# Graph attention over 2048 nodes: dense masked attention replaced by attention over gathered edges

## The reference, cut to what matters

```python
h  = relu(layernorm(x))                            # no scale or bias
hs = layer_norm(h, ln1)                            # source rows
ht = layer_norm(h_target, ln1)                     # target rows
q = (ht @ Wq + bq) / sqrt(32); k = hs @ Wk + bk; v = hs @ Wv + bv
logits = einsum('thd,shd->hts', q, k);  logits = where(adj != 0, logits, -1e30)
ctx  = softmax(logits) @ v                         # per head, 2048 x 256
ht   = ht + ctx @ Wo + bo
ht   = layer_norm(ht, ln2)
out  = x + ht + gelu(ht @ W1) @ W2                 # tanh form of gelu
```

## Time and profile before

| | before |
|---|---|
| median of 3 runs | 491.26 us (490.76 to 491.69) |
| profiled execution, span | 488.1 us |
| instructions | 10628 |
| PE busy | 472.1 us, 97% |
| DVE busy | 418.4 us, 86% |
| ACT busy | 376.5 us, 77% |
| POOL busy | 305.6 us, 63% |
| moved by DMA | 46.93 MB |

### The profile page before, as it was taken

How to read it: one execution, slowest core, us unless ns; L and a number is a source line. 1 busy time by engine, 2 the same in 40 slices (tenths; PEclk the granted TensorE clock), 3 DMA queues, 4 the chain that set the end, 5 groups by cost and what they waited for, 6 DMA issues and landing times.

```text
span 488.1 us, 10628 instructions
## 1 busy us (share of the span) xinstructions
PE 472.1 (97%) x4366; PEld 243.2 (50%) x4366; DVE 418.4 (86%) x631; ACT 376.5 (77%) x462; POOL 305.6 (63%) x152
## 2 busy tenths in 40 slices
PE   3999989999999999999999999999999999999995
PEld 1557533343333333343333333343435888888884
DVE  6889499999999999999999999999997977566243
ACT  4887979998998998998998998999995571727150
POOL 1000019977998999999999998999998300000000
PEclk9999999999999999999999999999999999999999
DMA  8997879925432673232763400500000100202021
GB/s 231 243 217 133 157 216 385 346 47 109 172 69 47 76 173 58 44 52 50 77 177 57 77 2 3 186 35 1 2 2 1 46 33 13 87 1 86 1 87 45
DMA packets 53775, 46.93 MB, mean 96 GB/s; under 512 B 35486, under 2 KB 46652, under 8 KB 53212
## 3 DMA queue, kind: packets, MB, share of 16 engines
q1 hardware_dynamic: 51216, 37.30, 28.7%
q0 software_dynamic: 2480, 8.92, 10.4%
q10 hardware_dynamic: 28, 0.01, 0.0%
HBM read 31.93 MB, written 14.81 MB: 96 GB/s over the span
## 4 chain that ended last, share of the span: by engine, by line
PE 72%; DVE 11%; issue 9%; ACT 4%; POOL 3%; DMA 1%; DVEq 0%; POOLq 0%
PE acc L1434 18%; PE slot L1419 16%; PE acc L1452 8%; DVE probs L1044 8%; PE slot L1536 3%; PE slot L1534 3%; PE slot L1535 3%; PE slot L1322 3%; PE acc L1571 2%; PE acc L1573 2%; PE acc L1572 2%; PE slot L1485 2%; POOL added_up L554 2%; DVE stats L865 1%; PE slot L1342 1%
## 5 line engine op out<-in xcount | busy, mean ns | idle before, releaser
L1044 DVE SCALAR_TENSOR_TENSOR probs<-maskT,slot 128x1024 f32<-128x1024 uint16 x256 | 298.0, 1217 | 6.1 <-PE slot L1419 5.7
L759 ACT ACTIVATE probs<-probs 128x1024 f32<-128x1024 f32 x256 | 266.8, 1057 | 22.3 <-DVE probs L1044 4.8
L554 POOL TENSOR_TENSOR added_up<-added_up,probs 128x1024 f32<-128x1024 f32 x96 | 226.8, 2411 | 0.2
L1434 PE MATMUL acc<-probs,V 128*32 128x512 f32 x1024 | 136.3, 604 | 1.8 <-DVE q_lo_staged L970 1.8
L1452 PE MATMUL acc<-probs,ones 128*32 128x256 f32 x1024 | 77.0, 379 | 0.0
L1452 PEld LDWEIGHTS acc<-probs,ones 128*32 128x32 f32 x1024 | 33.3, 110 | 72.8 <-issue 71.2
L1419 PE MATMUL slot<-q_hi,k_hi 32*128 32x512 f32 x512 | 64.4, 493 | 0.9 <-DVE probs L1044 0.3
L823 ACT ACTIVATE g_full<-slot 128x512 f32<-128x512 f32 x32 | 19.3, 602 | 45.2 <-issue 30.0
L1419 PEld LDWEIGHTS slot<-q_hi,k_hi 32*128 32x128 f32 x512 | 24.5, 181 | 59.1 <-DVE probs L1044 54.4
L551 POOL TENSOR_TENSOR added_up<-probs 128x1024 f32<-128x1024 f32 x16 | 38.1, 2406 | 24.9 <-ACT probs L759 15.0
L1419 PE MATMUL slot<-q_lo,k_hi 32*128 32x512 f32 x512 | 51.8, 391 | 0.0
(11 more groups left out here) (144 smaller groups left out, 496.6 us busy)
## 6 DMA issues: line engine op xcount, KB each, us to landing
adj_raw<-in_adj POOLq DMA_DIRECT2D x16, 512.0 KB, 5.5
htn<-in_L_gnn_h_target SPq DMA_DIRECT2D x4, 512.0 KB, 7.4
ht_saved<-htn SPq DMA_DIRECT2D x1, 2048.0 KB, 8.1
k_hi_saved<-k_hi SPq DMA_DIRECT2D x1, 2048.0 KB, 10.2
k_lo_saved<-k_lo SPq DMA_DIRECT2D x1, 2048.0 KB, 14.5
v_saved<-V SPq DMA_DIRECT2D x1, 2048.0 KB, 8.9
inverse<-inverse_saved SPq DMA_DIRECT2D x8, 256.0 KB
maskT<-in_L_gnn_W SPq DMA_DIRECT2D x2, 1024.0 KB, 6.4
```

The source lines that it names most:

```text
L554: nc.gpsimd.tensor_tensor(added_up[:, pair], added_up[:, pair], at(i), ALU.add).then_inc(added, 1)
L759: nc.scalar.activation(p, p, ACT.Exp).then_inc(exped, 1)
L1044: nc.vector.scalar_tensor_tensor(out=probs[:, u % RING], in0=m, scalar=-HALF_EDGE, in1=slot[u % SLOTS][:], op0=ALU.add, op1=ALU.min).then_ ...
L1434: mm = pe.matmul(acc[HD * j:HD * j + HD, 0, :], V[:, i, h * HD:(h + 1) * HD], probs[:, (PAIRS * k + j // 2) % RING, j % 2, :], start=(i == 0),
```

## The change

The names in the diff: P = 128, SLOTS = 11, KEYS = 24, REST = 13, RING = 2, WIDE = 264, ST = 16 tiles of 128 targets, NP = 8 pairs of tiles, ROUNDS = 20.

Keys and values are projected with rows in the partitions, joined to rows of 512 floats, and stored in HBM (`kv_saved`); queries stay in SBUF (`q_rows`). All products are plain fp32; the split parts go. The mask, its transposes and the dense scores go.

Per pair of tiles the adjacency becomes a list of sources: ACT squares it in place and counts it (`square`), PE packs 16 blocks of 128 columns as powers of two into one word per column (`put_in_words`), DVE takes the top exponent three times to turn a word into keys (`find_levels`), and sorts the 24 largest keys of a row with `max` of eight at a time and `match_replace` (`rank_keys`). A key's bits give the source's row (`make_index`). A row's first 11 sources are its slots. What is beyond them is moved to any of 128 shared lanes of the tile, one lane a source, through small products with a matrix of owners (`share_a`, `make_offsets`, `share_b`, `move_shared`, `share_c`).

Per tile POOL issues 12 indexed transfers of 128 rows of 2 KB (`gather`: 11 near, 1 far). From the third tile on an empty slot's index lies outside of the table, and its row isn't moved. Each round n then does the following. Every function named is one stream's part.

```diff
+            def gather(n):
+                if n < 2:
+                    for parity in range(2):
+                        pool.wait_ge(kv_stored[parity], 16 * NCH // 2)
+                else:
+                    pool.wait_ge(far_weighed, n - 1)
+                pool.wait_ge(indexed, 2 * (n // 2) + 2)
+                for s in range(SLOTS):
+                    pool.indirect_dma_start(
+                        out=near[:, n % RING, s, :], out_offset=None, in_=kv_saved,
...
+                pool.wait_ge(shared, SHARE_STEPS * (n // 2) + 13)
+                pool.indirect_dma_start(
+                    out=far[:, n % RING, :], out_offset=None, in_=kv_saved,
...
+            for n in range(ROUNDS):
+                if n + 1 < ST:
+                    gather(n + 1)
+                if n + FIRST_ADJ < ST:
+                    load_adj(n + FIRST_ADJ)
+                e = widened_in(n + 1)
+                if e is not None:
+                    root_pair(e)
...
+            def exponentials(n):
+                act.wait_ge(scored, SCORE_STEPS * (n + 1))
...
+                nc.scalar.activation(weights, logits[:].rearrange("p s h -> p (s h)"), ACT.Exp).then_inc(exped, 1)
+                nc.scalar.activation(values[:, :, D:WIDE], logits[:], ACT.Exp).then_inc(exped, 1)
...
+            for n in range(ROUNDS):
+                if n + FIRST_SQUARES < ST:
+                    square(n + FIRST_SQUARES)
+                if n < ST:
+                    exponentials(n)
+                if n + 1 < ST:
+                    place_query(n + 1)
+                e = widened_in(n)
+                if e is not None:
+                    norm_pair(e)
+                    gelu(e, (0, 1))
+                if 0 < n <= ST:
+                    copy_context(n - 1)
+                if e is not None:
+                    gelu(e, (2, 3))
+                if 0 < n <= ST:
+                    copy_y(n - 1)
...
+            def score(n):
...
+                nc.vector.tensor_tensor(products[:], near[:, n % RING, :, 0:D],
+                                        query_ps[:, None, :].to_broadcast([P, SLOTS, D]), ALU.mult).then_inc(scored, 1)
...
+                nc.vector.tensor_reduce(logits[:].rearrange("p s h -> p (s h)"),
+                                        products[:].rearrange("p s (h i) -> p (s h) i", i=HD), AX_X, ALU.add
+                                        ).then_inc(scored, 1)
...
+            def weigh(n):
...
+                nc.vector.tensor_tensor(values[:, :, 0:D].rearrange("p s (h i) -> p s h i", i=HD),
+                                        near[:, n % RING, :, D:2 * D].rearrange("p s (h i) -> p s h i", i=HD),
...
+            for n in range(ROUNDS):
+                if n < ST:
+                    score(n)
+                    far_score(n)
+                if 0 < n <= ST:
+                    divide(n - 1)
+                e = finished_in(n)
+                if e is not None:
+                    finish(e)
+                e = ranked_in(n)
+                if e is not None:
+                    find_levels(e)
+                    rank_keys(e)
+                    make_index(e)
+                    share_a(e)
+                e = shared_in(n)
+                if e is not None:
+                    share_b(e)
+                if n < ST:
+                    weigh(n)
+                if e is not None:
+                    share_c(e)
+                if 0 < n <= ST:
+                    measure(n - 1)
+                if n == ST:
+                    test_ranges()
                     make_flag()
...
+            def sum_up(n):
...
+                for s in range(SLOTS):
+                    pe.matmul(acc, ident[:], values[:, s, :], start=(s == 0), stop=False)
...
+                pe.matmul(acc, owner_T[:, n // 2 % 2, n % 2, :], far_values[:], start=False, stop=True
+                          ).then_inc(summed_up, 1)
...
+            for n in range(ROUNDS):
+                if 0 < n <= ST:
+                    sum_up(n - 1)
+                e = widened_in(n)
+                if e is not None:
+                    turn_y(e)
+                    widen(e, (0, 1))
+                o = narrowed_in(n)
+                if o is not None:
+                    narrow(o, 0)
+                if 0 < n <= ST:
+                    turn_context(n - 1)
+                s = shared_in(n)
+                if s is not None:
+                    move_shared(s)
+                if n + 1 < ST:
+                    spread_query(n + 1)
+                if 0 < n <= ST:
+                    attend(n - 1)
+                if e is not None:
+                    widen(e, (2, 3))
+                if o is not None:
+                    narrow(o, 1)
+                w = worded_in(n)
+                if w is not None:
+                    put_in_words(w)
```

The start changes with it. PE's `project(c)` makes keys and values tile by tile into two alternating PSUM places each, which ACT (`values_out`) and DVE (`keys_out`) empty. Pairs 0 and 1 are ranked before round 0, with the target rows' work in between:

```diff
             rectify_chunk(2)
+            source_affine(1)
             source_root(2)
             normalise_source(2)
+            values_out(1)
...
+            target_root(0)
+            values_out(3)
+            square(0)
+            square(1)
             normalise_target(0)
             target_root(1)
             normalise_target(1)
             target_affine(0)
+            square(2)
+            square(3)
             target_root(2)
+            normalise_target(2)
             target_affine(1)
             target_root(3)
+            normalise_target(3)
             target_affine(2)
+            square(4)
             target_affine(3)
+            place_query(0)
...
+            keys_out(3)
             target_scale(0)
+            find_levels(0)
+            rank_keys(0)
+            make_index(0)
+            share_a(0)
             target_stats(1)
...
             target_scale(3)
+            find_levels(1)
+            rank_keys(1)
+            make_index(1)
+            share_a(1)
+            queries_out(2)
+            queries_out(3)
```

More of the change, by code:

```diff
@@ new lines, in graph_attention @@
+        squared = sem("squared")
+        worded = sem("worded")
+        levels = sem("levels")
+        ranked = sem("ranked")
+        indexed = sem("indexed")
+        bounded = sem("bounded")
+        shared = sem("shared")
+        offset_made = sem("offset_made")
+        moved_made = sem("moved_made")
+        near_in = [sem(f"near_in{i}") for i in range(RING)]
+        far_in = [sem(f"far_in{i}") for i in range(RING)]
+        query_in = sem("query_in")
+        far_query_in = sem("far_query_in")
@@ L672, in values_out, with source_affine @@
-            def values_out(c):
-                act.wait_ge(v_projected, c + 1)
-                nc.scalar.copy(V[:, rows_of(c), :], slot4[2]).then_inc(v_out, 1)
+            def source_affine(c):
+                act.wait_ge(x_turned, c + 1)
+                if c == 0:
+                    act.wait_ge(columns_made, 1)
+                if c >= 2:
+                    act.wait_ge(kv_projected, TILES * (c - 1))
+                for d in range(DC):
+                    nc.scalar.activation(hsT[:, c % 2, d, :], wide[:, d, :], ACT.Identity, bias=beta1[:, d:d + 1],
+                                         scale=gamma1[:, d:d + 1]).then_inc(x_affine, 1)
@@ new lines, in values_out @@
+            def values_out(c):
+                if c == 0:
+                    act.wait_ge(nodes_made, 1)
+                if c >= 2:
+                    act.wait_ge(kv_stored[c % 2], 16)
+                for t in range(TILES):
+                    n = c * TILES + t
+                    act.wait_ge(kv_projected, n + 1)
+                    nc.scalar.activation(kv_out[:, c % 2, t, D:2 * D], turned[:, n % 2, 0:D], ACT.Copy,
+                                         scale=nodes[:, n:n + 1]).then_inc(v_out, 1)
@@ new lines, in target_affine @@
+                if c >= 2:
+                    act.wait_ge(q_projected, 2 * (c - 1))
+                for d in range(DC):
+                    nc.scalar.activation(htT[:, c % 2, d, :], wide[:, d, :], ACT.Identity, bias=beta1[:, d:d + 1],
+                                         scale=gamma1[:, d:d + 1]).then_inc(t_affine, 1)
+                for d in range(DC):
+                    nc.scalar.activation(ht2[:, d, cols_of(c)], wide[:, d, :], ACT.Identity,
+                                         bias=rest_col[:, d:d + 1], scale=gamma1[:, d:d + 1]).then_inc(t_affine, 1)
@@ L701, in _ @@
             act.wait_ge(made, 2)
-            nc.scalar.activation(warm[:], ones[:, 0:1], ACT.Sqrt).then_inc(warmed, 1)
+            nc.scalar.activation(warm[:], ident[:, 0:1], ACT.Sqrt).then_inc(warmed, 1)
             rectify_half(0)
@@ new lines, in gelu, with copy_context @@
+            def gelu(e, parts):
+                for f in parts:
+                    act.wait_ge(widened, FC // 2 * e + f + 1)
+                    if e and f == 0:
+                        act.wait_ge(narrowed, 2 * e)
+                    nc.scalar.activation(hidden[:, 2 * f:2 * f + 2, :],
+                                         wide[:, f % 2, :].rearrange("p (f t) -> p f t", f=2), ACT.Gelu_apprx_tanh
```

(19 more changed lines are left out.)

1713 lines of the change are left out of this document (734 added, 979 removed).

## The result

The changed kernel takes 522.0 us (520.1 to 522.7, four runs) against 491.0 (490.3 to 491.7, four runs) before: a ratio of 1.063, 95% interval 1.060 to 1.065. It is slower. The forecast was 462 within 425 to 500. Of its three terms the start was laid at 127 and came at 129 us (first `score`), the end at 35 and came at 36, the rounds at 297 and came at 354. All of the miss lies in the rounds, where the single operations of DVE and ACT cost about what was laid.

The account below looks back on a forecast made before the run. PE (97% busy) and DVE (86%) were taken to bound the old kernel together, its dense steps costing 297 us of PE. Start 127 + rounds 297 + end 35 = 459 us span, plus 3.2 gives 462, range 425 to 500.

Parts of the forecast that it names:

- the start: Everything before the first `score`: source and query projections, ranking of the first pairs, first gathers; laid at 127 us.
- the end: The tail from the last `weigh` to the final store; laid at 35 us.
- the rounds: Rounds 0 to 15 together, even ones at 15.3 and odd ones at 22.3 us; laid at 297 us.
- 11 g + 2 < 16.1 means g < 1.28 costs nothing: POOL's gather: with g us per indexed transfer, taken as 1.1, rows land before `score` needs them, at no cost.
- rival B: POOL sets the round: above 1.28 us per indexed transfer rounds lengthen, 483 us total at 1.5; chance 0.22.
- beneath DVE, if the clock holds: PE's work in the rounds: 31.7 us a pair of rounds, less than DVE's 37.4, at full clock.
- rival C: PE's clock falls in odd-round waits: 8 us more on the chain, seven times, 518 us total; chance 0.12.
- The odd chain: Odd round's sequence across ACT, PE and DVE from `score` to `measure`, ending at 22.3 us, level with DVE's 22.1.
- ACT's exponentials come at 6.3: Odd round: ACT's exponentials start 6.3 us in, when DVE's `score` is done, and end at 7.7.
- The 3.2 us put on top of the span: Difference between the old kernel's span, 488.1, and median run, 491.3, added to the forecast span of 459 us.
- Rival E: Each ACT table switch costs a load and as long again: 1.4 us, 13 times, 18 more, 480; chance 0.05.
- Rival D: Start and chain are shorter than laid: 3 us less an odd round, 10 less of the start, 430; chance 0.16.

Follow-up runs that it names:

- the fill: The changed kernel without indexed transfers from tile 2 on, plus unread identity products where PE idles in odd rounds from 5 on; 471.6 us, 0.960.
- nogather: The changed kernel without the indexed transfers of tiles 2 to 15, later tiles reusing the rows of tiles 0 and 1; 479.9 us, 0.976.
- root_in_ten: root_in_burst with SLOTS 10 instead of 11, so 11 indexed transfers a tile; 467.0 us, 0.953.
- root_in_burst: norm_first's order, with two transfers of an even tile's burst issued before POOL's `root_pair` and ten after; 480.7 us, 0.979.
- no_rows: The changed kernel with all indexed transfers issued, but from tile 2 on bounded so that almost no bytes move; 515.7 us, 1.051.
- norm_first: The changed kernel with the odd round's normalising put before ACT's exponentials and `turn_y` before PE's `sum_up`; 515.4 us, 1.052.
- root_in_pause: root_in_burst with POOL starting the burst for tile 15 only when that for tile 14 has landed; 480.6 us, 0.978.

## Why the prediction was wrong

**The step that failed** is POOL's: "11 g + 2 < 16.1 means g < 1.28 costs nothing". It asked only whether the rows are there when `score` wants them. They are, at a pitch of 1.31 (laid 1.1), where rival B's own formula would add some 4 us and the traces show no wait. But the issue had a second cost that no row before could show, a hold of PE's signals to other engines: 42 us between the measured times with and without the transfers, 44 of the rounds' 57 (354 less 310). No rival had it; B took POOL's time as POOL's alone.

**The other 13 us** (310 less 297) are "beneath DVE, if the clock holds". With the clock kept by the fill, the rounds came to 297, the number laid. That it agrees to the us is luck, since the parts differ: even rounds 14.9 for 15.3, full odd ones 23.1 for 22.3, and rounds 0, 1 and 14 shorter by 0.9 to 1.4. So rival C was real, with a third of its price: 2.7 us an odd round, not 8. In the changed kernel itself round 7's clock is 0.91. From 283.74 on it is 0.53 for 1.6 us, near the lower of its two levels, and the 16 instructions that start there take 5.41 us, for 3.62 at the upper level. The Trainium skill's page "TensorE: Matmul & The Clock Gate", Part 1, has an idle array fall to half; the trace agrees, after gaps of 2.1 and 1.1 us.

**The odd chain** was laid with one wait left out. "ACT's exponentials come at 6.3" overlooks that they write into `values`, which `sum_up` reads, so that they cannot start before it ends: 8.2 in `nogather`, 11.5 in the changed kernel (round 7 of both). That a chain laid from `score` on must begin with PE at rest was a second fault: PE carries 2.5 us (`nogather`) to 5.9 us of the even round over.

**Right**: the start and the end within 2 us, of the start with some luck, since it holds a hold too: the last copy of the queries comes 1.7 us behind PE's last product in the changed kernel, while the burst for tile 1 runs. The products' durations, and nearly the reduces'; bf16 products (16 in 1.9 us). The 3.2 us put on top of the span was too much: the profiled execution took 521.4 us with a span of 519.7, 1.7 more. Rival E is dead: a table load is 1.28 and the next instruction follows at once (in `root_in_ten` a load at 268.86, the gelu at 270.16). The Trainium skill's page "ScalarE: Activation LUTs", section "What ACT_TABLE_LOAD costs", would have 2.66; the measurement decides. Rival D did not come: the start was 2 us longer, not shorter.

**The chance** of slower was put at 0.18. The upper end of the range, 500, allowed for the unknown time of an instruction that no row showed, but not for an unknown effect of it on others, and B, C and the rest had been priced only one at a time.

What stays open: what inside the core makes the hold, and what sets its onset. The ends of PE's products are modelled in the profile, so the traces cannot tell a late signal from a product that itself completed late. In all runs, copies of `context` and `y` whose products ended less than 10 us into a burst were late by 1.8 us at most; of those more than 12 us into one, about two in three were late, by 1.2 to 6.5 us, and the others by less than 1, among them those of `root_in_burst`. The second gelu of round 13, 15 us into its run (at 424.9), was not late either. Whether a run of plain transfers as long as 15 us would hold too was not tried, nor a single transfer with several indices a row.

## What to carry to other kernels

An instruction that no trace has shown has two unknowns, its own time and what it does to its neighbours; take it out, or issue it and move nothing, before building a schedule on it. Long runs of indexed transfers on POOL should be placed where no other engine waits for PE: start them right behind the last such wait, keep them short, and put POOL's own small work into them. When two edits each bring nothing, look whether a loop joins them before dropping both: here 7 and 1 us alone were 41 together.

## What the hardware showed that was not expected

Bursts of twelve indexed transfers (1.01 us each, 0.30 between) held PE's signals to ACT and DVE by up to 6.5 us, and by 13 us in a run of 24 (from 429.3, the middle of `widen`'s second half in round 13, to 442.5); with nearly no bytes moved (`no_rows`) as well. In the changed kernel most of them came 1.5 to 1.9 us after the last transfer. That is no rule: in round 13 of `no_rows` and `norm_first` the held gelu started 4.3 and 7.0 us before the run of 24 was over. Signals between DVE and ACT were not seen to be late. Late in a run of 24, PE's own products came one by one, some 1.4 us apart, close to POOL's pitch of 1.31. And the first `score` came anywhere from 129 to 135 us in traces of kernels whose start is the same. Part of that is the same hold: the last copy of the queries came 1.4 to 3.1 us behind PE's last product in 15 traces and 0.04 us behind it in the three of `root_in_burst`, `root_in_pause` and `root_in_ten`. The rest is earlier, and no experiment looked into it.
